# Latent attention and a sign network on one core: queries projected two heads ahead, the row of reciprocals by transposes, the shift with one tensor operand

## The reference

```python
q_c = hidden_size @ Wq_c.T + bq_c
q = (q_c @ Wq_up.T + bq_up).reshape(b, s, NH, Q_HEAD).transpose(0, 2, 1, 3)
kv = hidden_size @ Wkv_c.T + bkv_c
kv_nope, kv_rope = (kv[..., :KV_LORA], kv[..., KV_LORA:])
kvu = (kv_nope @ Wkv_up.T + bkv_up).reshape(b, s, NH, QK_NOPE + V_HEAD).transpose(0, 2, 1, 3)
k_nope, v = (kvu[..., :QK_NOPE], kvu[..., QK_NOPE:])
k = jnp.concatenate([k_nope, jnp.broadcast_to(kv_rope...)], axis=-1)
scores = jnp.einsum('bhqd,bhkd->bhqk', q, k) / np.sqrt(Q_HEAD)
attn = jax.nn.softmax(scores, axis=-1)
o = jnp.einsum('bhqk,bhkv->bhqv', attn, v)
out = jnp.einsum('bhsv,Hv->bsH', o, Wo) + bo
```

## Time and profile before

| | |
|---|---|
| median of 3 runs | 1857.53 us (1855.07 to 1859.63) |
| the profiled execution | 1852.05 us, span 1850.2 us |
| PE busy | 1650.0 us (89%) |
| DVE busy | 1618.4 us (87%) |
| ACT busy | 1416.3 us (77%) |
| POOL busy | 969.6 us (52%) |
| DMA queue of SP, share of 16 engines | 87.1% |
| attention, first scores to last `onorm` | 97.96 to 1743.2 us |

### The profile page before, as it was taken

How to read it: one execution, slowest core, us unless ns; L and a number is a source line. 1 busy time by engine, 2 the same in 40 slices (tenths; PEclk the granted TensorE clock), 3 DMA queues, 4 the chain that set the end, 5 groups by cost and what they waited for, 6 DMA issues and landing times. The chain is left out here.

```text
span 1850.2 us, 23339 instructions
## 1 busy us (share of the span) xinstructions
PE 1650.0 (89%) x7316; PEld 753.7 (41%) x7316; DVE 1618.4 (87%) x2088; ACT 1416.3 (77%) x1979; POOL 969.6 (52%) x1355
## 2 busy tenths in 40 slices
PE   7988988998989889889989898898898988988799
PEld 6733333333333333333333333333333333333344
DVE  6679999999989999999989999999989999999565
ACT  5578888888878888888878888888878888888422
POOL 3246556565555565565555655555546555555320
PEclk9999999999999999999999999999999999999999
DMA  6599999999999999999999999999999999999611
GB/s 211 179 188 191 187 190 186 188 190 183 190 173 185 186 190 188 190 183 191 183 176 190 186 188 190 183 190 183 188 175 189 188 189 185 190 187 182 150 44 48
DMA packets 1092405, 330.84 MB, mean 179 GB/s; under 512 B 1070336, under 2 KB 1076768, under 8 KB 1092288
## 3 DMA queue, kind: packets, MB, share of 16 engines
q1 hardware_dynamic: 1080128, 296.22, 87.1%
q0 software_dynamic: 12160, 33.18, 6.6%
HBM read 50.39 MB, written 10.49 MB: 33 GB/s over the span
## 5 line engine op out<-in xcount | busy, mean ns | idle before, releaser
L969 DVE TENSOR_REDUCE mx<-S 128x1 f32<-128x1024 f32 x512 | 621.1, 1213 | 123.9 <-PE S L830 123.9
L925 ACT ACTIVATE S<-S,shift,unscale 128x1024 f32<-128x1024 f32 x512 | 602.0, 1176 | 158.0 <-DVE shift L975 145.9
L961 DVE TENSOR_TENSOR halves<-S,halves 128x1024 f16<-128x1024 f32 x512 | 621.6, 1214 | 2.6 <-ACT halves L934 2.6
L934 ACT ACTIVATE halves<-S 128x1024 f16<-128x1024 f32 x512 | 523.8, 1023 | 16.1
L828 PE MATMUL S<-kvTH,qeH 128*128 128x512 f16 x1024 | 392.2, 383 | 97.6 <-POOL qeL L740 93.2
L753 POOL TENSOR_TENSOR diagonal<-ident,recip 128x512 f32<-128x512 f32 x128 | 131.7, 1029 | 493.0 <-PE O L862 480.1
L830 PE MATMUL S<-kvTH,qeL 128*128 128x512 f16 x1024 | 388.1, 379 | 0.0
L829 PE MATMUL S<-kvTL,qeH 128*128 128x512 f16 x1024 | 388.1, 379 | 0.0
L840 PE MATMUL O<-PT,kvn 128*128 128x512 f16 x1024 | 243.6, 381 | 0.0
L975 DVE SCALAR_TENSOR_TENSOR shift<-mx,unscale,c_lift 128x1 f32<-128x1 f32 x512 | 225.8, 441 | 18.2
L828 PEld LDWEIGHTS S<-kvTH,qeH 128*128 128x128 f16 x1024 | 99.4, 97 | 332.1 <-POOL qeL L740 146.9
(11 more groups left out here) (263 smaller groups left out, 2018.6 us busy)
## 6 DMA issues: line engine op xcount, KB each, us to landing
weff<-weff_scratch POOLq DMA_DIRECT2D x126, 192.0 KB, 4.6
wv<-in_wv POOLq DMA_DIRECT2D x128, 64.0 KB, 3.1
PT<-halves SPq DMA_TRANSPOSE x512, 5.0
raw<-in_raw SPq DMA_DIRECT2D x8, 772.0 KB, 6.7
weff_scratch<-w_split SPq DMA_DIRECT2D x8, 768.0 KB, 5.2
x<-in_x SPq DMA_DIRECT2D x4, 1024.0 KB, 6.8
x_all<-in_x SPq DMA_DIRECT2D x3, 1024.0 KB, 5.6
out<-y SPq DMA_DIRECT2D x3, 1024.0 KB, 4.3
```

The costliest lines, as they stand in the source:

```text
L925: nc.scalar.activation(S[:, t % SLOTS, :], S[:, t % SLOTS, :], ACT.Exp, bias=shift[:, col:col + 1], scale=keep["unscale"][:, 0:1], accum_o ...
L934: nc.scalar.activation(halves[u][:, 0, :], S[:, t % SLOTS, :], ACT.Copy).then_inc(high_out, 1)
L961: v.tensor_tensor(halves[u][:, 1, :], S[:, t % SLOTS, :], halves[u][:, 0, :], ALU.subtract).then_inc(low_out, 1)
L969: v.reduce_max(mx[:, col:col + 1], S[:, t % SLOTS, :], AX.X).then_inc(max_ready, 1)
```

## The change

Queries are projected for step g+2 instead of g+1, in three buffers `qeH`/`qeL` taken by g % 3. `diagonal`, the square of ones and `osum` are gone: `repeat_row` is now four transposes of a reciprocal column repeated by a zero step, at the end of PE's step and for g-1; ACT copies the row to SBUF (`copy_row`, before exp of tile 3, two buffers), and `normalized` multiplies that row with bank `O` itself, during tile 0 of the next step. So bank `O` holds in a step: the values of g-2, the queries of g+2, the row of g-1. `values` waits for the row's copy. On POOL the load of weff is issued early in the step for g+3, and `split_q` last. The maximum is taken negated, and the shift is a tensor_scalar with one tensor and two scalars per partition.

```diff
         qef = [sb(f"qef{i}", [P, BLK]) for i in range(2)]
-        qeH = [sb(f"qeH{i}", [P, BLK], F16) for i in range(2)]
-        qeL = [sb(f"qeL{i}", [P, BLK], F16) for i in range(2)]
+
+        qeH = [sb(f"qeH{i}", [P, BLK], F16) for i in range(3)]
+        qeL = [sb(f"qeL{i}", [P, BLK], F16) for i in range(3)]
...
-        onorm, onormH, onormL, osum = (keep[n] for n in ("onorm", "onormH", "onormL", "osum"))
-        diagonal, square = sb("diagonal", [P, UN, P]), sb("ones_square", [P, P])
+        onorm, onormH, onormL = (keep[n] for n in ("onorm", "onormH", "onormL"))
+        row = [sb(f"recip_row{i}", [P, BLK]) for i in range(2)]
...
-            def split_q(nxt, i):
-                pool.wait_ge(q_copied, nxt + 1)
-                nc.gpsimd.tensor_copy(qeH[i][:], qef[i][:]).then_inc(q_high, 1)
-                pool.wait_ge(q_high, nxt + 1)
-                nc.gpsimd.tensor_tensor(qeL[i][:], qef[i][:], qeH[i][:], ALU.subtract).then_inc(q_low, 1)
-
-            split_q(0, 0)
-
-            def load_weights(g, weights, par):
-                pool.wait_ge(q_filled, g - 1)
-                pool.dma_start(f32(weff[par][:].rearrange("p t c -> p (t c)")), weights).then_inc(weff_next[par], 16)
-
-            def spread(g, i):
-
-                pool.wait_ge(recip_ready, g + 1)
-                if g:
-                    pool.wait_ge(row_filled, g)
-                nc.gpsimd.tensor_tensor(diagonal[:], ident[:].unsqueeze(1).broadcast_to((P, UN, P)),
-                                        recip[:, i * UN:(i + 1) * UN].unsqueeze(2).broadcast_to((P, UN, P)),
-                                        ALU.mult).then_inc(diagonal_ready, 1)
+            def split_q(k):
+                pool.wait_ge(q_copied, k + 1)
+                nc.gpsimd.tensor_copy(qeH[k % 3][:], qef[k % 2][:]).then_inc(q_high, 1)
+                pool.wait_ge(q_high, k + 1)
+                nc.gpsimd.tensor_tensor(qeL[k % 3][:], qef[k % 2][:], qeH[k % 3][:], ALU.subtract).then_inc(q_low, 1)
+
+            def load_weights(k):
+                pool.wait_ge(q_filled, k - 1)
+                pool.dma_start(f32(weff[k % 2][:].rearrange("p t c -> p (t c)")),
+                               dram["weff_h"][k % NH]).then_inc(weff_next[k % 2], 16)
+
+            load_weights(2)
+            split_q(0)
+            split_q(1)
 
             def body(g, b, h, par):
                 if exists(g):
                     if g >= 2:
                         pool.wait_ge(wv_split, g - 1)
                     pool.dma_start(wv[par][:], dram["wv"][h]).then_inc(wv_in[par], 16)
-                if exists(g - 1):
-                    spread(g - 1, 1 - par)
+                if exists(g + 3):
+                    load_weights(g + 3)
                 if exists(g - 2) and exists(g - 1):
...
-                if exists(g) and exists(g + 1):
-                    split_q(g + 1, 1 - par)
-                if exists(g + 2):
-                    load_weights(g + 2, dram["weff_h"][(h + 2) % NH], par)
                 if exists(g - 1):
...
+                if exists(g + 2):
+                    split_q(g + 2)
...
-            project_queries(0, 0, 0)
+            project_queries(0)
 
             for _ in range(8):
                 mm(S[:, SLOTS - 1, 0:BLK], keep["kvTH"][:, 0:P], keep["kvTH"][:, 0:BLK], start=True, stop=True)
+            pe.wait_ge(q_copied, 1)
+            project_queries(1)
...
-                        mm(out, qeH[par][:, q], keep["kvTH"][:, keys], start=True, stop=False)
-                        mm(out, qeH[par][:, q], keep["kvTL"][:, keys], start=False, stop=False)
-                        last = mm(out, qeL[par][:, q], keep["kvTH"][:, keys], start=False, stop=True)
+                        mm(out, qeH[g % 3][:, q], keep["kvTH"][:, keys], start=True, stop=False)
+                        mm(out, qeH[g % 3][:, q], keep["kvTL"][:, keys], start=False, stop=False)
+                        last = mm(out, qeL[g % 3][:, q], keep["kvTH"][:, keys], start=False, stop=True)
...
                 def values():
 
-                    if on:
-                        pe.wait_ge(q_copied, g + 1)
+                    if g >= 3:
+                        pe.wait_ge(onorm_ready, g - 2)
+                    pe.wait_ge(row_out, g - 1)
...
-                def repeat_row(out):
-
-                    pe.wait_ge(diagonal_ready, g - 1)
-                    mm(out, square[:], diagonal[:].rearrange("p u c -> p (u c)"), start=True, stop=True).then_inc(row_filled, 1)
-
-                def next_queries():
-                    if g >= 2:
-                        pe.wait_ge(onorm_ready, g - 1)
-                    project_queries(g + 1, (g + 1) // NH, 1 - par)
+                def repeat_row(k, out):
+
+                    pe.wait_ge(recip_ready, k + 1)
+                    for u in range(UN):
+                        at = k % 2 * UN + u
+                        last = nc.tensor.transpose(out[:, u * P:(u + 1) * P], recip[:, at:at + 1].broadcast_to((P, P)), ident[:])
+                    last.then_inc(row_filled, 1)
 
                 if on:
                     scores(0)
                 if g == NG:
                     pe.wait_ge(low_out, UN * NG - 1)
                     project_tile(UN - 1)
-                if g == NG + 1:
-
-                    repeat_row(S[:, 2, 0:BLK])
                 if exists(g - 2):
                     values()
                 if g == NG:
-                    pe.wait_ge(ones_set, 3)
-                    repeat_row(S[:, 2, BLK:2 * BLK])
+
+                    repeat_row(g - 1, S[:, 2, :])
                 if on:
                     scores(1)
-                    if g >= 2:
-                        pe.wait_ge(ones_set, 3)
-                        pe.wait_ge(o_out, g - 1)
-                        repeat_row(O[:])
                     scores(2)
-                    if exists(g + 1):
-                        next_queries()
+                    if exists(g + 2):
+                        if g >= 2:
+                            pe.wait_ge(onorm_ready, g - 1)
+                        else:
+                            pe.wait_ge(q_copied, g + 2)
+                        project_queries(g + 2)
...
                     output()
+                if on and exists(g - 1):
+
+                    if exists(g + 2):
+                        pe.wait_ge(q_copied, g + 3)
+                    elif g >= 2:
+                        pe.wait_ge(onorm_ready, g - 1)
+                    repeat_row(g - 1, O[:])
...
-                if exists(g - 2):
+                def copy_row(out):
+                    act.wait_ge(row_filled, g)
                     if g >= 3:
                         act.wait_ge(onorm_ready, g - 2)
-                    act.wait_ge(pv_done, g - 1)
-                    nc.scalar.activation(osum[:], O[:], ACT.Copy).then_inc(o_out, 1)
+                    nc.scalar.activation(row[1 - par][:], out, ACT.Copy).then_inc(row_out, 1)
+
                 if exists(g):
                     for u in range(UN):
-                        if u == 2 and exists(g + 1):
-                            copy_q(g + 1, (h + 1) % NH, 1 - par)
+                        if u == 2 and exists(g + 2):
+                            copy_q(g + 2)
+                        if u == 3 and exists(g - 1):
+                            copy_row(O[:])
                         exp(u)
                         high(u)
                 if g == NG:
+                    copy_row(S[:, 2, 0:BLK])
...
-                    v.reduce_max(mx[:, col:col + 1], S[:, t % SLOTS, :], AX.X).then_inc(max_ready, 1)
-
-                def negated(u):
+                    v.reduce_max(mx[:, col:col + 1], S[:, t % SLOTS, :], AX.X, negate=True).then_inc(max_ready, 1)
+
+                def shifted(u):
+
                     col = par * UN + u
                     at = slice(g * UN + u, g * UN + u + 1)
                     dve.wait_ge(max_ready, 4 * g + u + 1)
-                    v.scalar_tensor_tensor(out=shift[:, col:col + 1], in0=mx[:, col:col + 1], scalar=keep["unscale"][:, 0:1],
-                                           in1=keep["c_lift"][:, at], op0=ALU.mult, op1=ALU.subtract,
-                                           reverse1=True).then_inc(shift_ready, 1)
+                    v.tensor_scalar(shift[:, col:col + 1], mx[:, col:col + 1], keep["unscale"][:, 0:1],
+                                    keep["c_lift"][:, at], ALU.mult, ALU.add).then_inc(shift_ready, 1)
...
                 def reciprocals():
                     dve.wait_ge(probs_ready, UN * g)
                     if g >= 3:
-                        dve.wait_ge(diagonal_ready, g - 2)
+                        dve.wait_ge(row_filled, g - 2)
                     v.reciprocal(recip[:, (1 - par) * UN:(2 - par) * UN],
                                  rs[:, (1 - par) * UN:(2 - par) * UN]).then_inc(recip_ready, 1)
 
-                def normalized(row):
-                    dve.wait_ge(o_out, g - 1)
-                    dve.wait_ge(row_filled, g - 1)
+                def normalized():
```

(38 more changed lines are left out.)

## The result

The changed kernel takes 1743.39 us in the median of 4 runs (1741.29 to 1747.07), the kernel before 1858.38 beside it: a ratio of 0.9386, 95% interval 0.9364 to 0.9408. 1729 was forecast, 1714 to 1776 the range. The profiled execution took 1741.29 us.

A forecast was written before the change was run, and what follows sets the result against it. A ring of waits through all four engines was taken as the bound, 12.66 us a step; cut to 11.64, it saves 1.02 in 126 steps, 128.5 us: 1723.5 profiled, 1729 median, range 1714 to 1776.

The forecast's parts named there:

- The old ring: Chain of waits from onorm through queries, `qeL`, scores, values, maximum and shift back to onorm: 12.66 us, the whole step.
- the 0.55 us hold: Shift of tile 1 on DVE, held by POOL's `diagonal`: 0.77 us instead of 0.22 undisturbed.
- Queries ahead: Scores of step g+1 use queries made in step g-1, with a whole step of slack, cutting between `qeL` and scores.
- The new ring, 11.62: From copy_row over values, scores 1, maximum, shift, exp 1, query copy and exp 2 back to copy_row: 11.62 us a step.
- The 0.02 for neighbouring rings: Added to the 11.62 us step for rings 0.2 us and less below it, giving 11.64.
- its 1723.5: Forecast for the profiled execution in us: 1852.05 less 128.5, from 1.02 saved in each of 126 steps.
- (c): Rival: zero-step transposes on PE between output and scores 0 take 2.37 us for 0.60; +69 us, 1927; chance 0.06.
- The shift and POOL: The new one-tensor shift on DVE is not held by POOL's operations and always takes 0.22 us, bounds 0.15 and 0.77.
- (a): Rival: POOL still holds the new shift on DVE; 0.55 us more in the ring, 1798 us; chance 0.08.
- (b): Rival: the DMA engines are the bound and the change does nothing; step stays 12.66 us, 1857 us; chance 0.05.
- My 10.9 us for a step's transfers: DMA time needed per step, taking 1.01 / 1.17 as the busy part; under the 11.64 us step.

## Why the prediction was right, and where it was off

**The old ring**: right. Taking the 0.55 us hold out of it, by an edit on DVE or by another on POOL and PE, shortened the typical step by 0.49 and 0.54.

**Queries ahead**: right, and the whole of the effect, taken together with the row's new place. Alone it gives 0.938, with the other two 0.939. The shift and the row, worth 68 and 74 us alone, add nothing to it here: once the old ring is cut, the step is the new ring, and there only a shift of tile 1 held at that moment counts. Without the new shift but with the transposes it is held (12.00), with `diagonal` in POOL's order it mostly falls at the end of a cast (11.67). So the new shift is worth 0.27 beside the transposes; beside `diagonal` in the new order it was not run. I had priced the shift at 0.55 in the ring; undone, it cost 0.27, since of onormL only a part still lay ahead of it.

**The new ring, 11.62**: the right one, mis-sized by 0.11. The terms: the shift with two scalars per partition takes 0.27, not 0.22 (+0.05); the handoff from copy_row to values 0.10, not 0.05; the rest 0.01. I had taken the shift's length from the old form and bounded it below by 0.15; that row has a constant for a scalar. The 0.02 for neighbouring rings was not needed. 126 times the 0.09 over 11.64 is 11 us.

**Irregular steps**: not in my sum. The steps' mean is 0.14 over the typical one after, 0.06 before: 17 against 7 us over 127 intervals. Two kinds stand out. At each change of block PE waits for DVE, and the row and its copy stand behind that; the three changes, with the step behind each, cost 12.0 us over typical steps after and 8.0 before. And a late transpose holds PE, with 4.6 us over three steps. PE and ACT at the first change of block, then PE at the late transpose:

```profile
513.19 1.12 PE L893 MATMUL V<-ones_row,bv 32*128 32x512 f32 x2 [0.74 <-DVE x L986]
...
516.48 0.60 ACT L940 ACTIVATE recip_row<-O 128x512 f32<-128x512 f32 x1 [2.69 <-PE O L860]
```

```profile
371.42 3.11 PE L836 MATMUL O<-PT,kvn 128*128 128x512 f16 x8 [2.03 <-DMA PT<-halves]
```

Two stretches behind the late transpose (us, then PE, PEld, DVE, ACT, POOL busy, clock, DMA share, GB/s):

```profile
372.00:374.00 2.00, 2.00 (x7) 0.60 (x4) 1.45 (x3) 1.94 (x4) 0.00 (x0) 0.50 1.20 317
...
376.00:378.00 2.00, 2.00 (x10) 0.88 (x9) 1.30 (x2) 0.00 (x0) 1.18 (x2) 1.00 1.14 210
```

Before the first of these PE had waited 2.03 us for the transpose, and the granted clock is 0.50 there, the 1.2 GHz level; the step took 15.2. At the change of block it is 0.50 as well from 516 to 518 us, after PE had idled 0.90 and 0.74.

**The sum against the time.** The profiled execution missed its 1723.5 by 17.8 us (1741.29). The ring gives 11 of them and the irregular steps 10, together 21; the head gave 1.2 back and the tail nothing, and 127 intervals instead of 126, from 12.67 instead of 12.66, give back 2 more. The medians differ by only 14.4, and those 3.4 us are luck: I had carried over the 5.5 us between profiled execution and median of the kernel before, and after the change it was 2.1. In (c), the ring with transposes of 2.37 comes to 13.24 to 13.27 by its own terms, not 13.2, so its price was 73 to 77 us, not 69; nothing else hangs on it.

**The shift and POOL**: right. All 512 new shifts take 271 to 277 ns. Of these 126 begin under onormL's 1.27 us, 119 of them with more of it left than they take; in the kernel with the new shift alone 125 lie under `diagonal`. In the kernel before the 125 shifts begun under `diagonal` all take 0.77, and end 15 to 22 ns after it. The Trainium skill, "SBUF — State Buffer", the two separate sides, has GpSimd and a VectorE operation with two SBUF inputs hold a shared port pair exclusively, each for its whole instruction; these rows agree. The Trainium skill, "VectorE: DVE Perf Modes", what auto-detection checks, gives a 2-port mode to one-source operations in SBUF whose outermost non-unit dimensions are both even or equal, which would suggest the same hold for the new shift; at one element per partition none shows it.

**Rivals**: (a) did not happen. (c) did not: four zero-step transposes take 0.65; eight of them cost nothing and twelve 0.25. (b) was wrong for the change, but was the next layer: 0.5 us below this ring, late transposes already take most of a gain (0.48 us of a typical step, 0.17 of the mean). My 10.9 us for a step's transfers, from busy share alone, said nothing of a single transfer landing after 9.8 instead of 5.2 us.

## What to carry to other kernels

Close the chain before counting savings: a step is as long as its longest ring of waits, and an edit that shortens a ring which another edit has cut adds nothing to it. Sum the ring that comes next with durations of the very form of instruction that the change uses, and give the irregular steps a term of their own: they cost 7 us in the kernel before, 17 in the changed one and 56 with `values` after scores 1. When a typical step improves and the mean doesn't, look at the tail of the transfers' landing times and leave out a load to see what it costs.

## What was not expected of the hardware

- A one-element tensor_scalar with two scalars per partition takes 0.27 us, the scalar_tensor_tensor with two tensors 0.22; only the second was held by POOL (0.77 under `diagonal`, ended 15 to 22 ns after it).
- A weff load of 192 KB a step beside the transposes costs 0.38 us a step in the mean (11.69 to 11.31; 0.42 by the medians of the runs), while the DMA share from 400 to 1200 us is 1.11 with it and 1.08 without; moving it within the step changed nothing (1725.15 and 1723.45). What makes the transposes late, and what part the issue on POOL has in it, was not tried.
- Putting the wait that ends last behind four fulfilled ones on PE lengthened the handoff from 0.10 to 0.14 (medians 0.098 and 0.145).
